# A two-layer graph network on one core: split aggregate, another order of first slot and drain, first load in halves

## Chip, core and metric

One core of a Trainium2 chip runs the whole kernel. The metric is the device time of one execution in microseconds.

## What is computed

64 graphs of 128 nodes with 256 features, in fp32. Each graph goes through two attention layers, each with a residual and a layer norm:

```python
# layer 0
q, k = split(x @ Wqk); v = x @ Wv0
agg = einsum('bij,bjd->bid', adj, k * mask)
w = 1/16 * mask * einsum('bid,bid->bi', q, agg)
x1 = layernorm(x + softmax(w, axis=1)[:, :, None] * v)
# layer 1
query = x1 @ Wq.T + bq; key = x1 @ Wk.T + bk; value = x1 @ Wv.T + bv
weight = adj * exp(query @ key.T)
weight = weight / sum(weight, axis=2)
out = layernorm(x1 + weight @ value)
```

## The kernel before

The graphs are taken in 32 pairs. Weights are folded first: M0 = Wq0 Wk0^T / 16 and A = Wk1^T Wq1, so that layer 0 needs x M0 and x Wv0 (one product of 512 columns, `project_half`), the masked adjacency times x (`aggregate`), and layer 1 needs z = A x1 (`queries`), the scores (`scores`), the values (`values`) and the weighted sum (`attend`). Products that must be exact to nearly fp32 are made of three fp32r products: each operand is split into a high part, which is a cast to fp32r, and a low part, which is what is left. `split_half` (L747) issues hi x hi, hi x lo, lo x hi. `aggregate` (L758), `scores`, `attend` and the transposes are plain fp32 products; for fp32 of 256 columns the trace has two matmul records to a product.

The order is written by hand, for each engine on its own, in a function `slot(t, r)`. The slots -2 to 29 are run in turn, 4 to 27 as a loop unrolled by four, and `drain` comes behind them. In slot t the engines work on pairs t-1 to t+4 at once. TensorE's order in a slot (L884):

- transposes of x1 of pair t (L822)
- aggregate and projection, first graph, of pair t+2 (L765, L748 to L750)
- attend of pair t-1 (L845)
- projection, second graph, of pair t+2
- queries of pair t
- transpose of the row w of pair t+2 (L791)
- values and scores of pair t
- transpose of the softmax row p of pair t+2 (L797)

VectorE (L640): p_col copy and x1_sum of pair t+1 (L544, L549), edge of t-1 (L651: exp(scores) times adj, two inputs from SBUF), the high and low part of x1t (L537, L539), statistics and variance, row weights w of t+2 (L524), x2 of t-1 (L691), its statistics, the row maximum (L703), the reciprocal and the product p_row of t+2 (L711), the score bias of t (L717).

ScalarE (L448): exponentials of the scores of t-1 (L403), copy of x1t of t (L458), copy of agg of t+2 (L464), high part of xt of t+3 (L390), norm of x2 of t-3 and of x1 of t+1 (L396), z bias of t (L409), row exponential of t+2 (L490) into exp_row in SBUF, value copy of t (L503).

GpSimd (L328): rstd and shift of the two norms (L336, L339), low part of xt of t+3 (L344), x1b = x1 + value bias of t+1 (L275), mask of adjacency t+3 (L267).

SyncE issues all transfers in one queue. At the start: wqk (512 KB), xt(0), wv0, adj(0), x(0), the parameters of layer 1, and so on.

The words slot, pair and half are used in this sense below. PSUM has 8 banks: x1t and z share bank 0, scores and sums banks 1 and 2, the values 3 and 4, the projection 5 and 6 (with the rows w and p in the same banks), the aggregate 7.

```python
def split_half(out, s_hi, s_lo, m_hi, m_lo, first, last):
    nc.tensor.matmul(out, s_hi, m_hi, start=first, stop=False)
    nc.tensor.matmul(out, s_hi, m_lo, start=False, stop=False)
    return nc.tensor.matmul(out, s_lo, m_hi, start=False, stop=last)
```

## Time and profile before

| | |
|---|---|
| median of 3 runs | 312.04 us (311.88 to 312.27) |
| profiled execution | 311.97 us, span 310.1 us |
| TensorE matmul busy | 298.0 us, 96% |
| weight loads busy | 269.3 us, 87% |
| VectorE | 223.6 us, 72% |
| ScalarE | 195.8 us, 63% |
| GpSimd | 143.2 us, 46% |
| 16 DMA engines | 32.8% of their time, 31.26 MB |

The span runs from the first to the last instruction; the run's own time has about 2 us around it. Matmuls overlap one another, so a matmul's own length is more than its step to the next; the time that a series takes is read from starts. An engine's idle time is put down to what ended it, in square brackets.

### The profile page before, as it was taken

The numbers are of one execution on the slowest core, as the hardware profiler recorded it, in microseconds if no ns is written. First come the engines' busy times: TensorE is split into PE (matmuls) and PEld (weight loads), VectorE is DVE, ScalarE is ACT, GpSimd is POOL, SyncE is SP. The second block draws the span as 40 slices with busy tenths as digits, with TensorE's granted clock in tenths as the row PEclk, the third lists the DMA queues.
The fourth block names the chain that finished last, engine by engine and source line by source line (L and its number), as shares of the span: only waits on it lengthen the run. The fifth ranks groups of instructions, "written<-read, shape, count | busy, mean of one in ns | idle before, by whom it ended". The sixth has DMA issues, their size and how long they took to land. (4 is left out here: it accounts for less than half of the span.)

```text
span 310.1 us, 6526 instructions
## 1 busy us (share of the span) xinstructions
PE 298.0 (96%) x1900; PEld 269.3 (87%) x1900; DVE 223.6 (72%) x691; ACT 195.8 (63%) x453; POOL 143.2 (46%) x181
## 2 busy tenths in 40 slices
PE   8997999999999999999999999999999999999891
PEld 6876999999998999999998999999999999999780
DVE  2475778777778877777788777778877777788565
ACT  4354556676666666766666676666666766665761
POOL 2365554345555444455543345555443455542522
PEclk9999999999999999999999999999999999999997
DMA  6921224232434332234333222444423234210012
GB/s 231 327 71 35 85 88 116 52 113 83 118 119 119 119 91 80 80 105 119 119 119 111 83 73 90 118 119 119 119 85 83 81 107 119 85 53 36 34 36 101
DMA packets 19165, 31.26 MB, mean 101 GB/s; under 512 B 2128, under 2 KB 6608, under 8 KB 19152
## 3 DMA queue, kind: packets, MB, share of 16 engines
q1 hardware_dynamic: 19152, 31.11, 32.8%
q8 instruction: 6, 0.10, 0.1%
q14 instruction: 7, 0.06, 0.1%
HBM read 22.71 MB, written 8.39 MB: 100 GB/s over the span
## 5 line engine op out<-in xcount | busy, mean ns | idle before, releaser
L336 POOL TENSOR_TENSOR rstd<-var_eps,minus_half 128x4 f32<-128x4 f32 x31 | 31.5, 1018 | 138.6 <-DVE var_eps L669 124.5
L396 ACT ACTIVATE x<-x_sum,shift,rstd 128x256 f32<-128x256 f32 x62 | 34.0, 595 | 52.2 <-POOL shift L339 52.2
L748 PE MATMUL ps<-w_hi,xt_hi 128*128 128x512 f32 x128 | 61.6, 481 | 0.5 <-DVE w_lo L734 0.5
L750 PE MATMUL ps<-w_hi,xt_lo 128*128 128x512 f32 x128 | 50.4, 394 | 0.0
L749 PE MATMUL ps<-w_lo,xt_hi 128*128 128x512 f32 x128 | 50.2, 393 | 0.0
L275 POOL TENSOR_TENSOR x1b<-x,bv_all 128x512 f32<-128x512 f32 x32 | 41.5, 1297 | 4.3 <-DVE x L568 3.1
L344 POOL TENSOR_TENSOR xt_lo<-xt_raw,xt_hi 128x512 fp32r<-128x512 f32 x31 | 40.0, 1291 | 3.3 <-ACT xt_hi L390 3.3
L748 PE MATMUL ps<-wv_hi,x1t_hi 128*128 128x258 f32 x124 | 37.8, 304 | 0.0
L396 ACT ACTIVATE x<-x,shift,rstd 128x256 f32<-128x256 f32 x62 | 33.8, 595 | 3.5 <-POOL shift L287 3.5
L750 PE MATMUL ps<-wv_hi,x1t_lo 128*128 128x258 f32 x124 | 35.3, 285 | 0.0
L748 PE MATMUL ps<-x1t_hi,at_hi 128*128 128x256 f32 x124 | 35.1, 283 | 0.0
L749 PE MATMUL ps<-wv_lo,x1t_hi 128*128 128x258 f32 x124 | 35.1, 283 | 0.0
L749 PE MATMUL ps<-x1t_lo,at_hi 128*128 128x256 f32 x124 | 35.0, 282 | 0.0
L750 PE MATMUL ps<-x1t_hi,at_lo 128*128 128x256 f32 x124 | 34.8, 281 | 0.0
L409 ACT ACTIVATE z<-ps,z_bias 128x256 f32<-128x256 f32 x62 | 26.0, 470 | 11.3 <-PE ps L750 11.3
L524 DVE CUSTOM_DVE_ANT_0 agg<-ps,agg,adjt 128x256 f32<-128x256 f32 x64 | 30.9, 484 | 2.9 <-PE ps L750 0.8
L765 PE MATMUL ps<-x_raw,adjm 128*128 128x256 f32 x128 | 32.9, 380 | 0.0
L840 PE MATMUL ps<-x1t,z 128*128 128x128 f32 x240 | 31.8, 275 | 0.6 <-ACT z L409 0.6
L845 PE MATMUL ps<-val,edge 128*128 128x258 f32 x124 | 32.1, 380 | 0.0
L549 DVE SCALAR_TENSOR_TENSOR x_sum<-ps,p_col,x_raw 128x256 f32<-128x256 f32 x64 | 28.0, 479 | 3.2
L840 PEld LDWEIGHTS ps<-x1t,z 128*128 128x128 f32 x240 | 29.3, 191 | 0.8 <-ACT z L409 0.8
L748 PEld LDWEIGHTS ps<-w_hi,xt_hi 128*128 128x128 f32 x128 | 24.1, 188 | 5.7 <-issue 0.9
(121 smaller groups left out, 668.8 us busy)
## 6 DMA issues: line engine op xcount, KB each, us to landing
xt_raw<-xt_pairs SPq DMA_DIRECT2D x32, 256.0 KB, 2.7
x_raw<-x_pairs SPq DMA_DIRECT2D x32, 256.0 KB, 2.7
out_pairs<-x SPq DMA_DIRECT2D x31, 256.0 KB, 2.1
adjt<-adjt_pairs SPq DMA_DIRECT2D x32, 129.0 KB, 2.1
...
```

What stands on the lines that cost most here:

```text
L275: nc.gpsimd.tensor_tensor(x1b[r % 2][:, :].rearrange("p (g d) -> p g d", g=2), x1[r % 2][:, :].rearrange("p (g d) -> p g d", g=2), bv_all[ ...
L336: nc.gpsimd.tensor_tensor(rstd[r % 2][:, :, :], var_eps[:, :, :], minus_half[:, :, :], ALU.pow)\
L344: nc.gpsimd.tensor_tensor(xt_lo[(r + 3) % 2][:, :, :, :].rearrange("p t g n -> p (t g n)"), xt_raw[(r + 3) % 2][:, :], xt_hi[(r + 3) % 2][ ...
L396: last = nc.scalar.activation(out[:, graph(g)], in_[:, graph(g)], ACT.Identity, bias=shift[r % 2][:, layer, g:g + 1], scale=rstd[r % 2][:, ...
L524: nc.vector.tensor_tensor_reduce(agg[:, g, :], y_ps(r)[:, g, :], agg[:, g, :], adjt[r % 4][:, PAIR_N + g:PAIR_N + g + 1], 0.0, ALU.mult, A ...
L549: nc.vector.scalar_tensor_tensor(out=x1_sum[r % 2][:, graph(g)], in0=v0_ps(r)[:, g, :], scalar=p_col[:, g:g + 1], in1=x_raw[r % 4][:, grap ...
L748: nc.tensor.matmul(out, s_hi, m_hi, start=first, stop=False)
L749: nc.tensor.matmul(out, s_hi, m_lo, start=False, stop=False)
L750: return nc.tensor.matmul(out, s_lo, m_hi, start=False, stop=last)
L765: mm = nc.tensor.matmul(agg_ps[:, g, :], adjm[r % 2][:, graph(g, NODES)], x_raw[r % 4][:, graph(g)], start=True, stop=True)
L840: mm = nc.tensor.matmul(out[:, g, :], zs[:, k, graph(g, NODES)], xs[:, k, g, :], start=(k == 0), stop=(k == HALVES - 1))
L845: return nc.tensor.matmul(out[:, g, 0:VAL_COLS], edges[:, graph(g, NODES)], vals[:, g, :], start=True, stop=True)
```

## The change

It has four parts.

1. Split aggregate. For pairs 4 to 31 (SPLIT = 4) `aggregate` is a `split_product` of adjm and x. ScalarE makes the high parts (`split_adjm`, `split_x`), GpSimd the low parts (`low_adjm`, `low_x`), in new buffers. GpSimd's mask moves from the end of the slot to behind the shift. Pairs 0 to 3 keep the fp32 product.
2. First slot. The bias products, transposes of w and p, the z bias on ScalarE, the x1 transposes and GpSimd's x1b stand in another order in the start and in slot 0. The transposes of x1 are now issued at the end of a slot (`transpose_next`), which in other slots is the same place. exp_row lies in PSUM.
3. Drain. Pair 30 gets its own z, val and edge instead of pair 31, and its values, scores and attend come earlier.
4. First load. The host lays out wqk by halves of the contracted dimension, two transfers of 256 KB load it, and M0's products wait for the half that they need. ScalarE issues xt(0).

```diff
+SPLIT = 4
...
+        def exp_row_ps(r):
+            return yv_ps(r)[0:2, 0, NODES:2 * NODES]
...
-            sp.dma_start(p0[:, 0:4 * DIM], params0[:, 0:4 * DIM]).then_inc(wqk_loaded, 16)
-            load_xt(0, 0)
+            for k in range(HALVES):
+                c = graph(k, 2 * DIM)
+                sp.dma_start(p0[:, c], params0[:, c]).then_inc(wqk_loaded[k], 16)
...
+            def low_adjm(u, r):
+                pool.wait_ge(adjm_hi_done, u + 1 - SPLIT)
+                nc.gpsimd.tensor_tensor(adjm_lo[r % 2][:, :], adjm[r % 2][:, :],
+                                        adjm_hi[r % 2][:, :].bitcast(F32), ALU.subtract).then_inc(adjm_lo_done, 1)
+
+            def low_x(u, r):
+                pool.wait_ge(x_hi_done, u + 1 - SPLIT)
+                nc.gpsimd.tensor_tensor(x_lo[r % 2][:, :], x_raw[r % 4][:, :],
+                                        x_hi[r % 2][:, :].bitcast(F32), ALU.subtract).then_inc(x_lo_done, 1)
+
             def slot(t, r):
+                if exists(t + 3) and r + 3 >= SPLIT:
+                    low_x(t + 3, r + 3)
                 if exists(t + 1) or exists(t - 2):
...
+                if exists(t + 3) and r + 3 >= SPLIT:
+                    mask_adj(t + 3, r + 3)
...
                 if r == -2:
                     mask_adj(1, 1)
                     mask_adj(2, 2)
-                if r == -1:
                     pool.wait_ge(wv1_hi_done, 1)
                     nc.gpsimd.tensor_tensor(wv1_lo[:, :, 0:DIM], wv1T, wv1_hi[:, :, 0:DIM].bitcast(F32), ALU.subtract)\
                         .then_inc(wv1_lo_done, 1)
+                if r == -1:
+                    mask_adj(3, 3)
+                    pool.wait_ge(x1t_lo_done, 1)
                 if exists(t + 1):
...
-                if exists(t + 3) and r >= 0:
-                    mask_adj(t + 3, r + 3)
+                if exists(t + 3) and r + 3 >= SPLIT:
+                    low_adjm(t + 3, r + 3)
...
+            def split_x(u, r):
+
+                act.wait_ge(x_loaded[r % 4], transfers4(u, r))
+                act.wait_ge(agg_done, u - 1)
+                nc.scalar.copy(x_hi[r % 2][:, :], x_raw[r % 4][:, :]).then_inc(x_hi_done, 1)
+
+            def split_adjm(u, r):
+
+                act.wait_ge(adjm_done, u + 1)
+                act.wait_ge(agg_done, u - 1)
+                nc.scalar.copy(adjm_hi[r % 2][:, :], adjm[r % 2][:, :]).then_inc(adjm_hi_done, 1)
+
...
                 act.wait_ge(z_done, a + 1)
-                bias_z(z)
+                bias_z(z_a)
+                act.wait_ge(val_done, a + 1)
+                nc.scalar.copy(val_a[:, :, 0:DIM], val_ps[:, :, 0:DIM]).then_inc(val_copied, 1)
                 normed_out(DRAIN - 1, n + 1)
-
-                act.wait_ge(x1t_lo_done, b + 1)
-                nc.scalar.copy(x1t[:, :, :, :], x1t_drain_ps).then_inc(x1t_copied, 1)
-                act.wait_ge(val_done, a + 1)
-                nc.scalar.copy(val[:, :, 0:DIM], val_ps[:, :, 0:DIM]).then_inc(val_copied, 1)
-                act.wait_ge(z_done, b + 1)
-                bias_z(z_b)
                 act.wait_ge(score_done, a + 1)
                 act.wait_ge(score_bias_done, a + 1)
                 act.wait_ge(edge_done, a)
-                exp_scores(score_ps)
+                exp_scores(score_a_ps)
+
+                act.wait_ge(x1t_lo_done, b + 1)
+                nc.scalar.copy(x1t[:, :, :, :], x1t_drain_ps).then_inc(x1t_copied, 1)
+                act.wait_ge(z_done, b + 1)
+                bias_z(z)
                 act.wait_ge(val_done, b + 1)
-                nc.scalar.copy(val_b[:, :, 0:DIM], val_ps[:, :, 0:DIM]).then_inc(val_copied, 1)
+                nc.scalar.copy(val[:, :, 0:DIM], val_ps[:, :, 0:DIM]).then_inc(val_copied, 1)
                 act.wait_ge(score_done, b + 1)
                 act.wait_ge(score_bias_done, b + 1)
                 act.wait_ge(edge_done, b)
-                exp_scores(score_b_ps)
+                exp_scores(score_ps)
...
+                if r == 0:
+                    act.wait_ge(z_done, 1)
+                    act.wait_ge(biases_ready, 1)
+                    bias_z(z)
...
                                          accum_out=exp_sum[:, 0:1]).then_inc(row_exp_done, 1)
+                if exists(t + 3) and r + 3 >= SPLIT:
+                    split_adjm(t + 3, r + 3)
...
+                if exists(t + 4) and r + 4 >= SPLIT:
+                    split_x(t + 4, r + 4)
...
+            act.dma_start(xt_raw[0][:, :], xt_pairs[0]).then_inc(xt_loaded[0], 16)
...
                 sum_x1(b, b)
+                bias_scores(DRAIN)
...
+                bias_scores(a)
                 dve.wait_ge(sum_done, DRAIN + 1)
                 attended(DRAIN, sum_ps)
-                bias_scores(a)
+                weigh_edges(a, edge_a)
                 dve.wait_ge(x2_done, DRAIN + 1)
                 both_stats(1, x2[DRAIN % 4]).then_inc(stats2_done, 1)
                 dve.wait_ge(stats2_done, DRAIN + 1)
                 dve.wait_ge(shift_done, n + 1)
                 variance(1)
-                weigh_edges(a, edge)
-                bias_scores(b)
-                weigh_edges(b, edge_b)
 
                 dve.wait_ge(sum_done, a + 1)
-                attended(a, sum_ps)
+                attended(a, sum_a_ps)
                 dve.wait_ge(x2_done, a + 1)
                 both_stats(1, x2[a % 4]).then_inc(stats2_done, 1)
                 dve.wait_ge(stats2_done, a + 1)
                 dve.wait_ge(shift_done, n + 2)
                 variance(1)
-
-                dve.wait_ge(last_sum_done, 1)
-                attended(b, sum_b_ps)
+                bias_scores(b)
+                weigh_edges(b, edge)
+
+                dve.wait_ge(sum_done, b + 1)
+                attended(b, sum_ps)
...
-                    dve.wait_ge(bias_done, 1)
-                    nc.vector.tensor_copy(z_bias[:, :], bias_ps[:, 0:HALVES])
-                    nc.vector.tensor_copy(s_bias[:, :], bias_ps[:, HALVES:HALVES + 1]).then_inc(biases_ready, 1)
...
+                if r == -1:
+                    dve.wait_ge(bias_done, 1)
+                    nc.vector.tensor_copy(z_bias[:, :], bias_ps[:, 0:HALVES])
+                    nc.vector.tensor_copy(s_bias[:, :], bias_ps[:, HALVES:HALVES + 1]).then_inc(biases_ready, 1)
...
-                    nc.vector.tensor_scalar(p_row[0:2, :], exp_row[:, :], inv_sum[:, 0:1], None, ALU.mult)\
+                    nc.vector.tensor_scalar(p_row[0:2, :], exp_row_ps(r + 2), inv_sum[:, 0:1], None, ALU.mult)\
...
+                if r < SPLIT:
+                    pe.wait_ge(adjm_done, u + 1)
+                    pe.wait_ge(x_loaded[r % 4], transfers4(u, r))
+                else:
+                    pe.wait_ge(adjm_lo_done, u + 1 - SPLIT)
+                    pe.wait_ge(x_lo_done, u + 1 - SPLIT)
                 if exists(u - 1):
                     pe.wait_ge(agg_copied, u)
                 for g in range(2):
-                    mm = nc.tensor.matmul(agg_ps[:, g, :], adjm[r % 2][:, graph(g, NODES)], x_raw[r % 4][:, graph(g)],
-                                          start=True, stop=True)
+                    n = graph(g, NODES)
+                    if r < SPLIT:
+                        mm = nc.tensor.matmul(agg_ps[:, g, :], adjm[r % 2][:, n], x_raw[r % 4][:, graph(g)],
+                                              start=True, stop=True)
+                    else:
+                        mm = split_product(agg_ps[:, g, :], [(adjm_hi[r % 2][:, n], adjm_lo[r % 2][:, n],
+                                                              x_hi[r % 2][:, graph(g)], x_lo[r % 2][:, graph(g)])])
...
+                    if r == 2 and g == 0 and k == 0:
+                        transpose_p(1, 1)
...
                 values(x1t_hi_a, x1t_lo_a, 0)
+                values(x1t_hi_a, x1t_lo_a, 1).then_inc(val_done, 1)
...
-                values(x1t_hi_a, x1t_lo_a, 1).then_inc(val_done, 1)
+                pe.wait_ge(z_copied, a + 1)
+                scores(score_a_ps, z_a, x1t_a)
 
                 pe.wait_ge(x1t_lo_done, b + 1)
-                pe.wait_ge(z_copied, a + 1)
                 queries(x1t_hi, x1t_lo)
-                pe.wait_ge(x2_done, DRAIN + 1)
-                scores(score_ps, z, x1t_a)
+                pe.wait_ge(edge_done, a + 1)
                 pe.wait_ge(val_copied, a + 1)
+                attend(sum_a_ps, edge_a, val_a, 0)
+                attend(sum_a_ps, edge_a, val_a, 1).then_inc(sum_done, 1)
                 pe.wait_ge(score_bias_done, a + 1)
                 values(x1t_hi, x1t_lo, 0)
                 values(x1t_hi, x1t_lo, 1).then_inc(val_done, 1)
                 pe.wait_ge(z_copied, b + 1)
                 pe.wait_ge(x1t_copied, b + 1)
-                scores(score_b_ps, z_b, x1t)
-                pe.wait_ge(edge_done, a + 1)
+                pe.wait_ge(x2_done, DRAIN + 1)
+                scores(score_ps, z, x1t)
+                pe.wait_ge(edge_done, b + 1)
+                pe.wait_ge(val_copied, b + 1)
                 attend(sum_ps, edge, val, 0)
                 attend(sum_ps, edge, val, 1).then_inc(sum_done, 1)
-                pe.wait_ge(edge_done, b + 1)
-                pe.wait_ge(val_copied, b + 1)
-                attend(sum_b_ps, edge_b, val_b, 0)
-                attend(sum_b_ps, edge_b, val_b, 1).then_inc(last_sum_done, 1)
+
+            def transpose_next(t, r):
+                pe.wait_ge(x1_done, t + 2)
+                if r == -1:
+                    pe.wait_ge(biases_ready, 1)
+                else:
+                    pe.wait_ge(z_copied, t + 1)
+                transpose_x1(x1t_ps, r + 1)
...
-                if r == 0:
-                    transpose_p(1, 1)
...
-                if exists(t + 2):
+                if exists(t + 2) and r > 0:
                     transpose_w(t + 2, r + 2)
...
+                    if r == 0:
+                        transpose_w(2, 2)
...
-                if exists(t + 2) and r != DRAIN:
+                if r == 0:
+                    transpose_next(t, r)
                     transpose_p(t + 2, r + 2)
+                elif r != DRAIN:
+                    transpose_p(t + 2, r + 2)
+                    transpose_next(t, r)
...
-            pe.wait_ge(wqk_loaded, 16)
             for m in range(HALVES):
                 for k in range(HALVES):
-                    mm = nc.tensor.matmul(m0_ps[:, m, :], wqkT[:, k, m * 128:(m + 1) * 128], wqkT[:, 2 + k, :],
+                    pe.wait_ge(wqk_loaded[k], 16)
+                    mm = nc.tensor.matmul(m0_ps[:, m, :], wqkT[:, 2 * k, m * 128:(m + 1) * 128], wqkT[:, 2 * k + 1, :],
...
-            fold_biases()
+            aggregate(1, 1)
             transpose_p(0, 0)
-            aggregate(1, 1)
             project(1, 1, 0)
             project(1, 1, 1)
+            fold_biases()
+            transpose_w(1, 1)
             aggregate(2, 2)
-            transpose_w(1, 1)
+            transpose_next(-1, -1)
```

On GpSimd, one slot of the loop. Before (rstd and shift of the norms, xt_lo of pair t+3, x1b of t+1, mask of t+3):

```order
L336 TENSOR_TENSOR rstd<-var_eps,minus_half 128x4
L339 TENSOR_TENSOR shift<-neg_mean,rstd 128x4
L344 TENSOR_TENSOR xt_lo<-xt_raw,xt_hi 128x512
L275 TENSOR_TENSOR x1b<-x_0,bv_all 128x512
L267 TENSOR_TENSOR adjm<-adjt 128x256
```

And now:

```order
L343 TENSOR_TENSOR x_lo<-x_raw,x_hi 128x512
L356 TENSOR_TENSOR rstd<-var_eps,minus_half 128x4
L359 TENSOR_TENSOR shift<-neg_mean,rstd 128x4
L275 TENSOR_TENSOR adjm<-adjt 128x256
L366 TENSOR_TENSOR xt_lo<-xt_raw,xt_hi 128x512
L283 TENSOR_TENSOR x1b<-x_0,bv_all 128x512
L338 TENSOR_TENSOR adjm_lo<-adjm,adjm_hi 128x256
```

Two subtractions are new, at the slot's two ends, and the mask stands ahead of xt_lo.

On ScalarE, from the copy of x1t(0) in slot 0 on. Before (z is the z bias, x_1 the norm of x1, exp_row the row exponential):

```order
L458 COPY x1t<-ps 128x512
L464 COPY agg<-ps 128x512
L390 CAST xt_hi<-xt_raw 128x512
L396 ACTIVATE x_1<-x_sum,shift,rstd 128x256 x2
L409 ACTIVATE z<-ps,z_bias 128x256 x2
L490 ACTIVATE exp_row,exp_sum<-ps,neg_max 2x128
L503 COPY val<-ps 128x2x256
L403 ACTIVATE exp_s<-ps,score_bias 128x128 x2
```

And now:

```order
L494 COPY x1t<-ps 128x512
L500 COPY agg<-ps 128x512
L414 CAST xt_hi<-xt_raw 128x512
L445 ACTIVATE z<-ps,z_bias 128x256 x2
L432 ACTIVATE x_1<-x_sum,shift,rstd 128x256 x2
L528 ACTIVATE ps,exp_sum<-ps,neg_max 2x128
L543 COPY val<-ps 128x2x256
L421 CAST x_hi<-x_raw 128x512
L439 ACTIVATE exp_s<-ps,score_bias 128x128 x2
```

The z bias stands ahead of the norm, and the cast of x ahead of the score exponentials. From slot 1 on the cast of adjm stands between the row exponential and the value copy as well.

On VectorE, the end of the drain (x_2 is x2 of pair 30, x_3 of pair 31). Before:

```order
L558 TENSOR_SCALAR neg_mean<-stats 128x2
L559 TENSOR_SCALAR var_eps<-stats 128x2
L555 TENSOR_TENSOR edge<-exp_s,adjt 128x256
L575 TENSOR_SCALAR score_bias<-ps,s_bias 128x2
L555 TENSOR_TENSOR edge_b<-exp_s,adjt 128x256
L563 RECIPROCAL den_inv<-ps 128x2
L568 SCALAR_TENSOR_TENSOR x_2<-ps,den_inv,x1b 128x256 x2
L530 BN_STATS stats<-x_2 128x6
L558 TENSOR_SCALAR neg_mean<-stats 128x2
L559 TENSOR_SCALAR var_eps<-stats 128x2
L563 RECIPROCAL den_inv<-ps 128x2
L568 SCALAR_TENSOR_TENSOR x_3<-ps,den_inv,x1b 128x256 x2
```

And now:

```order
L601 TENSOR_SCALAR neg_mean<-stats 128x2
L602 TENSOR_SCALAR var_eps<-stats 128x2
L606 RECIPROCAL den_inv<-ps 128x2
L611 SCALAR_TENSOR_TENSOR x_2<-ps,den_inv,x1b 128x256 x2
L573 BN_STATS stats<-x_2 128x6
L601 TENSOR_SCALAR neg_mean<-stats 128x2
L602 TENSOR_SCALAR var_eps<-stats 128x2
L618 TENSOR_SCALAR score_bias<-ps,s_bias 128x2
L598 TENSOR_TENSOR edge<-exp_s,adjt 128x256
L606 RECIPROCAL den_inv<-ps 128x2
L611 SCALAR_TENSOR_TENSOR x_3<-ps,den_inv,x1b 128x256 x2
```

The last edge product stands behind all of pair 30's work, and only its own den_inv and x2 follow it.

## Rows read from the trace of the kernel before

**Rows 1.** Stretches view: PE, PEld, DVE, ACT, POOL busy us, clock, DMA share, GB/s.
```profile
80.00:160.00 80.00, 80.00 (x520) 72.97 (x520) 60.49 (x189) 54.09 (x126) 38.13 (x44) 1.00 0.34 102
```

**Rows 2.** Timeline, TensorE, one slot of the loop (start, length, engine, line).
```profile
146.15 0.27 PE L797 MATMUL ps<-ident,p_row 128*128 128x128 f32 x1
...
151.20 0.28 PE L748 MATMUL ps<-x1t_hi,at_hi 128*128 128x256 f32 x1
...
152.63 0.27 PE L791 MATMUL ps<-ident,w_col 128*2 128x128 f32 x1
...
155.09 0.27 PE L797 MATMUL ps<-ident,p_row 128*128 128x128 f32 x1
...
155.63 0.38 PE L765 MATMUL ps<-x_raw,adjm 128*128 128x256 f32 x1
...
156.73 0.39 PE L749 MATMUL ps<-w_lo,xt_hi 128*128 128x512 f32 x1
...
156.96 0.40 PE L750 MATMUL ps<-w_hi,xt_lo 128*128 128x512 f32 x1
```

**Rows 3.** Timeline, GpSimd, ScalarE and the edge product, same slot.
```profile
150.05 1.02 POOL L336 TENSOR_TENSOR rstd<-var_eps,minus_half 128x4 f32<-128x4 f32 x1 [4.50 <-DVE var_eps L669]
...
153.81 0.61 POOL L267 TENSOR_TENSOR adjm<-adjt 128x256 f32<-128x256 f32 x1
...
153.81 0.18 ACT L490 ACTIVATION_READ_ACCUMULATOR exp_row<-ps,neg_max 2x1 f32 x1
...
154.40 0.59 ACT L503 COPY val<-ps 128x512 f32<-128x512 f32 x1 [0.41 <-PE ps L750]
...
155.32 0.62 ACT L403 ACTIVATE exp_s<-ps,score_bias 128x128 f32<-128x128 f32 x2 [0.34 <-PE ps L840]
...
156.46 0.41 DVE L651 TENSOR_TENSOR edge<-exp_s,adjt 128x256 f32<-128x256 f32 x1
```

**Rows 4.** Groups by form: line, shapes, count, busy us, mean ns of one.
```profile
L344 POOL TENSOR_TENSOR xt_lo<-xt_raw,xt_hi 128x512 fp32r<-128x512 f32 x31 | 40.0, 1291 | 3.3 <-ACT xt_hi L390 3.3
...
L390 ACT CAST xt_hi<-xt_raw 128x512 fp32r<-128x512 f32 x32 | 19.9, 623 | 3.8 <-DMA xt_raw<-xt_pairs 3.8
...
L510 ACT CAST w_hi<-p 128x256 fp32r<-128x256 f32 x2 | 0.7, 402 | 0.0
```

**Rows 5.** One line each, VectorE: shortest, median and longest ns, first and last start.
```profile
L734 DVE TENSOR_TENSOR w_lo<-p,w_hi x2: 415/624/834, 7.1 to 7.4; 128x256 fp32r<-128x256 f32 x2
...
L537 DVE CAST x1t_hi<-x1t x30: 418/420/1427, 20.9 to 282.1; 128x512 fp32r<-128x512 f32 x30
...
L711 DVE TENSOR_SCALAR p_row<-exp_row,inv_sum x32: 273/289/723, 13.6 to 288.5; 2x128 f32<-2x128 f32 x32
```

**Rows 6.** Timeline, ScalarE and TensorE, end of slot 0.
```profile
27.54 0.82 ACT L409 ACTIVATE z<-ps,z_bias 128x256 f32<-128x256 f32 x2
...
28.25 0.34 ACT L490 ACTIVATE exp_row<-ps,neg_max 2x128 f32<-2x128 f32 x1
...
29.77 0.30 PE L797 MATMUL ps<-ident,p_row 128*128 128x128 f32 x1 [0.21 <-DVE p_row L711]
...
30.36 0.38 PE L765 MATMUL ps<-x_raw,adjm 128*128 128x256 f32 x1
```

**Rows 7.** Timeline, TensorE and VectorE, the drain.
```profile
288.91 0.30 PE L797 MATMUL ps<-ident,p_row 128*128 128x128 f32 x1
...
289.73 0.22 DVE L717 TENSOR_SCALAR score_bias<-ps,s_bias 128x2 f32<-128x2 f32 x1 [0.96 <-ACT val L503]
...
302.08 1.14 PE L845 MATMUL ps<-val_b,edge_b 128*128 128x258 f32 x4 [0.33 <-DVE edge_b L555]
...
304.03 0.16 DVE L563 RECIPROCAL den_inv<-ps 128x2 f32<-128x2 f32 x1
```

**Rows 8.** Timeline, ScalarE and TensorE, the first projection.
```profile
6.63 0.71 ACT L510 CAST w_hi<-p 128x256 fp32r<-128x256 f32 x2
...
7.64 0.47 PE L748 MATMUL ps<-w_hi,xt_hi 128*128 128x512 f32 x1 [0.49 <-DVE w_lo L734]
```

45 lines of the change are left out of this document (18 added, 27 removed).

## The prediction

> **What bounds the kernel now.** I read the table of stretches first [rows 1]. TensorE is busy for the whole 80 us of a stretch in the middle; the list of waits names none of TensorE's between 40 and 270 us, and its clock there is granted in full. VectorE and ScalarE are busy three quarters and two thirds of that stretch, GpSimd under half. So in the loop only TensorE's own work counts, as long as no other engine becomes late. Second, one slot of the loop on TensorE [rows 2]: from one transpose of the softmax row (L797) to the next, 8.94 us. Third, the same slot on GpSimd and ScalarE, for their free time [rows 3]. Last, the two ends of the program, where TensorE does wait [rows 6 to 8].
>
> **The aggregate, 28 of 32 pairs.** Before, one aggregate is two fp32 products, four matmul records. The first starts at 155.63; the projection behind it has its second record at 156.73, and records of that shape follow at 0.23 us (156.73 to 156.96), so the projection began at 156.50: four passes take 0.87 us, 0.2175 each [rows 2]. After, it is six fp32r products of 128x256. Twelve of just that shape, the queries, run from 151.20 to 152.63: 0.119 each, six take 0.715 [rows 2]. Gain 0.155 us a slot. Pairs 4 to 31 are changed, so 28 x 0.155 = **4.3 us**, and the slot becomes 8.785 us. Everything else on TensorE in the loop stays in the same order: the x1 transposes stood behind the softmax transpose already, only in the next slot's text.
>
> **What pays for it on ScalarE.** Two casts a slot. The half of adjm (128x256) takes 0.40 us, of x (128x512) 0.62 [rows 4]. The first goes behind the row exponential, whose accumulator read ends at 153.99 (153.81 + 0.18), and before the value copy at 154.40, which waits for TensorE: 0.41 us are free and 0.40 wanted [rows 3]. The second goes behind the value copy (154.40 + 0.59), before the score exponentials at 155.32. Two copies follow each other about 0.1 us before the first has ended, so it runs about 154.9 to 155.5 and the exponentials start 0.1 us late. Behind them ScalarE waits for the aggregate anyway. I cost both at nothing. If that cover failed, the score bias and the column copy behind it on VectorE would be late, and with them x1_sum, for which the projection waits.
>
> **What pays for it on GpSimd.** The subtraction for x (128x512) costs 1.29 us, that for adjm half, 0.65 [rows 4]. GpSimd's new order is: low half of x, rstd, shift, mask, xt_lo, x1b, low half of adjm. The last is what the next aggregate waits for. From the start of rstd at 150.05 to that of the mask at 153.81 lie 3.76 us (rstd, shift, xt_lo, x1b) [rows 3]; with mask 0.61 and the new 0.65 the chain ends at 155.07. The aggregate's weights are wanted 0.1 us before its first pass, now at 146.15 + 8.785 + 0.54 - 0.1 = 155.38 (0.54 from L797 at 155.09 to L765 at 155.63) [rows 2]. So 0.3 us of slack, the narrowest place of the change. The low half of x ends soon after its cast, about 156.9, two microseconds before rstd of that slot; alone it costs nothing.
>
> It does collide with VectorE. Two VectorE subtractions of one shape at the start, with GpSimd's first mask beside them, took 415 and 834 ns; the cast of x1t takes 420 ns, and 1427 once, in slot 0, when GpSimd's x1b ran beside it; the p_row product 273 to 723 [rows 5]. The low half of x (155.6 to 156.9) lies over the edge product, which ran at 156.46 in this slot [rows 3]. Held until 156.9, that ends about 0.3 us later, with it x1t_hi, x1t_lo, the statistics, the variance and rstd: the slack of 0.3 is used up, to within a tenth. The page "SBUF — State Buffer" of the Trainium skill, section "Who interferes with whom", states it harder: a VectorE instruction with two SBUF inputs and a GpSimd one that reads SBUF exclude each other for the whole instruction. The pair 415/834 agrees with that. By the page the edge product waits for all that is left of the subtraction, which is what I have just counted. Taken as strictly for x1t_hi and x1t_lo it makes rivals 1 and 4, and by rival 1 the time would be 307.5 us instead of 304.7.
>
> I take no loss in the loop, with bounds of 0 and 2.8 us (a tenth of a microsecond in each of 28 slots). exp_row goes to PSUM and p_row is read from there. That is the same count of elements, and in the loop TensorE transposes p_row when its own order comes to it, not when p_row is ready: nothing for it there.
>
> **The start.** Before, the first aggregate of a full slot (pair 3) starts at 30.36 us, behind the transposes of p_row(2) at 29.77 and of x1 [rows 6]. What led to 29.77 was: x_sum(1), its statistics, norm of x1(1), then the z bias on ScalarE (27.54), then the row exponential (28.25), then p_row. The change shortens it four times. GpSimd's x1b now waits for x1t_lo, so x1t_hi isn't held: 1.43 to 0.42, 1.0 us [rows 5]. The z bias goes ahead of the norm, so the exponential follows the norm directly: 28.25 - 27.54 = 0.7 us [rows 6]. p_row, 723 ns in that slot, is no longer held by the mask: 0.45 us [rows 5]. The x1 transposes (0.4 us) are issued ahead of p_row's, in its wait. Against it: the projection of pair 3 must still wait for x_sum(2), which now starts after the short path; I take 0.3 us back. 1.0 + 0.7 + 0.45 + 0.4 - 0.3 = **2.3 us** (2.25, rounded). The w transpose, for which TensorE waited in slot 0, now stands behind the values and is covered by them; that is the same time and isn't counted twice. The bias matmuls go behind projection 1 and hide in TensorE's wait for w_col(1). Bounds: 1.5 (another wait takes one of the steps), 3.0.
>
> **The first loads.** The first half of wqk lands earlier and the fold M0 begins earlier. But the first projection (7.64) follows the cast of wv0 (6.63) and its subtraction [rows 8], and wv0's transfer is still third in SyncE's queue with the same bytes before or beside it, xt(0) now on ScalarE's. Nothing gained. Bounds -0.4 and +0.3: an issue's time either way.
>
> **The drain.** The last pair's result waits on VectorE today: its attend is four passes from 302.08 on, about 0.9 us, so done and visible at 303.2; but its den_inv starts at 304.03, behind pair 30's x2, statistics and variance [rows 7]. The new order gives pair 30 its own edge, z and val early and takes its x2 before the last edge: **0.7 us**, at most 0.8 from this. The other part: score_bias(29) at 289.73 stood before p_col, though p_row was transposed from 288.91 [rows 7]; that start comes 0.5 us earlier, but TensorE must then first finish values of pair 30 (now both graphs ahead of the x1 transposes), so little of it passes through. Bounds 0 and 1.3.
>
> **Sum.** 4.3 + 2.3 + 0.7 = 7.3 us. The profiled execution took 311.97 us, 0.07 under the median of 312.04; either way **304.7 us**. A measurement of this kernel tells about 0.2% (0.6 us) from no change. Own range of this case: gains of 9.3 (4.6 + 3.0 + 1.3 + 0.4) to 5.4: 302.7 to 306.6.
>
> **Rivals.**
> 1. *The aggregate waits for GpSimd's low half of adjm.* For it: slack of 0.3 us against a delay of 0.3. Against it: the chain starts with the softmax transpose that ends one slot and is waited for in the slot after the next transpose, so it spans two slots, and each loses half of what it is late by. 0.1 us a slot takes 2.8 of the 4.3 back: 307.5 us. Chance 0.18.
> 2. *The start stays as long*, since another chain (norm of x1, x_sum(2)) ends there as late as before: 304.7 + 2.3 = 307.0 us. Chance 0.07.
> 3. *The split saves nothing*: six weight loads instead of four, and the switch between fp32 and fp32r passes, cost the 0.155 us. The queries show the rate, but not between fp32 neighbours. 312.0 - 3.0 = 309.0 us. Chance 0.06.
> 4. *Slower: GpSimd becomes the bound.* The place is the low half of x. If x1t_hi or x1t_lo, not edge alone, is held by it for a full 1.29 us, rstd is late by that, and low adjm by 1.29 - 0.3 = 1.0. The chain spans two slots, so a slot loses 0.5: 8.785 + 0.5 = 9.28 against 8.94 is 0.34 x 28 = 9.5 us more, less 3.0 from the ends: 318.5 us. It decides as slower from 0.26 us lost in a slot (0.155 + 3.0/28), that is a delay over 0.8 us of that chain. Against it: the cast of x ends before the exponentials, so GpSimd has long begun. By the same section of the Trainium skill whoever starts first holds the port; here GpSimd starts first and is nearly done. Chance 0.05.
> 5. *No change*: rivals 1 and 3 together with a lost start. 312 us. Chance 0.02.
>
> The forecast has 0.62. Faster: 0.62 + 0.18 + 0.07 + 0.06 = 0.93; within 0.2%: 0.02; slower 0.05. The range holds the forecast's own without its utmost gain and reaches to rivals 1 and 2: 303.2 to 307.6 us.
>
> **What the new profile would show.** Right: L797's successor every 8.78 us in the middle; six fp32r records of 0.12 us for an aggregate; TensorE with no wait on GpSimd's adjm_lo or x_lo; the aggregate of pair 3 at about 28 us; den_inv of the last pair behind TensorE, not behind VectorE's own work. Wrong: idle of TensorE before the aggregate, released by GpSimd (rivals 1, 4); edge or x1t_hi in the loop of over 0.8 us; a slot still 8.94 us with TensorE busy throughout (rival 3); a first projection later than 7.9 us.

## The result, and the profile after

The changed kernel takes 305.15 us (median of 4 runs, 304.99 to 305.53), the kernel before 311.96 us in the same comparison; ratio 0.978, 95% interval 0.977 to 0.980. The forecast was 304.7 us in a range of 303.2 to 307.6. The profiled execution is the longest of the four, 305.53 us with a span of 303.7 us.

The table of stretches after the change, same stretch and columns as [rows 1]:

```profile
80.00:160.00 80.00, 80.00 (x546) 73.98 (x546) 62.84 (x190) 61.08 (x146) 56.90 (x65) 1.00 0.34 103
```

TensorE is still busy throughout, with more records (546 for 520). GpSimd has paid: 56.90 us for 38.13. The waits of 40 to 270 us (us in total, times, longest) name no TensorE wait; the first rows are

```profile
POOL rstd L356 <- DVE var_eps L713: 61.6, 26, 2.4
ACT x L432 <- POOL shift L359: 50.2, 26, 2.9
DVE inv_sum L752 <- ACT ps L528: 21.0, 26, 0.8
```

One slot of the loop on TensorE (timeline; start, length), to be set against [rows 2]. L851 is the transpose of p_row, L876 those of x1, and L791 to L793 the three lines of the split product:

```profile
142.54 0.27 PE L851 MATMUL ps<-ident,p_row 128*128 128x128 f32 x1
...
151.36 0.27 PE L851 MATMUL ps<-ident,p_row 128*128 128x128 f32 x1
151.47 0.60 PE L876 MATMUL ps<-ident,x 128*128 128x128 f32 x4
151.83 0.38 PE L791 MATMUL ps<-x_hi,adjm_hi 128*128 128x256 f32 x1
152.04 0.28 PE L792 MATMUL ps<-x_lo,adjm_hi 128*128 128x256 f32 x1
152.16 0.28 PE L793 MATMUL ps<-x_hi,adjm_lo 128*128 128x256 f32 x1
...
152.52 0.28 PE L793 MATMUL ps<-x_hi,adjm_lo 128*128 128x256 f32 x1
152.64 0.40 PE L791 MATMUL ps<-w_hi,xt_hi 128*128 128x512 f32 x1
152.88 0.40 PE L792 MATMUL ps<-w_lo,xt_hi 128*128 128x512 f32 x1
```

Five of the six products start 0.12 us before their successor, as forecast; the first has 0.21. Not all of that is the first product's own: its record starts 0.03 us behind that of the last of the four transposes (151.80), and transposes follow each other at 0.11 us. The whole place, from the last transpose's start to the second record of the projection, took 156.73 - 155.53 = 1.20 us before and takes 152.88 - 151.80 = 1.08 now. The slot takes 8.82 us. From the transpose of p_row(3) to that of p_row(30), 27 slots, before: (280.42 - 38.74) / 27 = 8.951 us; after: (274.90 - 36.60) / 27 = 8.826 us. So a slot gained 0.125 us, not 0.155. Most slots take 8.79 to 8.83 us; the five in which the loop turns (in which its body of four slots starts again) take 8.97, 8.92, 8.91, 8.89 and 8.89.

The same slot on GpSimd and VectorE, which answers to [rows 3]:

```profile
143.03 1.29 POOL L343 TENSOR_TENSOR x_lo<-x_raw,x_hi 128x512 fp32r<-128x512 f32 x1
143.90 0.71 DVE L695 TENSOR_TENSOR edge<-exp_s,adjt 128x256 f32<-128x256 f32 x1
...
146.72 1.02 POOL L356 TENSOR_TENSOR rstd<-var_eps,minus_half 128x4 f32<-128x4 f32 x1 [2.40 <-DVE var_eps L713]
147.82 0.20 POOL L359 TENSOR_TENSOR shift<-neg_mean,rstd 128x4 f32<-128x4 f32 x1
147.97 0.61 POOL L275 TENSOR_TENSOR adjm<-adjt 128x256 f32<-128x256 f32 x1
148.54 1.28 POOL L366 TENSOR_TENSOR xt_lo<-xt_raw,xt_hi 128x512 fp32r<-128x512 f32 x1
149.79 1.28 POOL L283 TENSOR_TENSOR x1b<-x,bv_all 128x512 f32<-128x512 f32 x1
...
151.03 0.74 POOL L338 TENSOR_TENSOR adjm_lo<-adjm,adjm_hi 128x256 fp32r<-128x256 f32 x1
```

The low part of x runs over the edge product, which ends 0.3 us late (0.71 for 0.41 us), and the low part of the masked adjacency ends at 151.77, 0.05 us before the aggregate's first weight load at 151.82. On this way the slack of 0.3 us is used up, as worked out.

The start, which answers to [rows 6], and the drain, to [rows 7]:

```profile
20.97 0.43 DVE L580 CAST x1t_hi<-x1t 128x512 fp32r<-128x512 f32 x1 [0.53 <-ACT x1t L494]
...
24.66 0.84 ACT L445 ACTIVATE z<-ps,z_bias 128x256 f32<-128x256 f32 x2 [2.72 <-PE ps L793]
25.63 1.09 ACT L432 ACTIVATE x<-x_sum,shift,rstd 128x256 f32<-128x256 f32 x2
26.63 0.30 ACT L528 ACTIVATE ps<-ps,neg_max 2x128 f32<-2x128 f32 x1
...
27.28 0.34 DVE L756 TENSOR_SCALAR p_row<-ps,inv_sum 2x128 f32<-2x128 f32 x1
...
27.77 0.30 PE L851 MATMUL ps<-ident,p_row 128*128 128x128 f32 x1 [0.25 <-DVE p_row L756]
27.91 0.88 PE L814 MATMUL ps<-x_raw,adjm 128*128 128x256 f32 x3
...
296.38 1.14 PE L899 MATMUL ps<-val,edge 128*128 128x258 f32 x4 [1.25 <-DVE edge L598]
...
297.56 0.17 DVE L606 RECIPROCAL den_inv<-ps 128x2 f32<-128x2 f32 x1 [1.23 <-PE ps L899]
```

p_row(2) is transposed at 27.77 (before 29.77), and the aggregate of pair 3 starts at 27.91. The last pair's den_inv now waits for TensorE; TensorE's last product itself waits 1.25 us for VectorE's last edge product, where it waited 0.33 before [rows 7]. Where the span's 6.4 us come from: up to p_row(3) 38.74 - 36.60 = 2.14, the 27 slots 241.68 - 238.30 = 3.38, and from p_row(30) to the end 29.68 - 28.80 = 0.88, of which 0.13 is the last split aggregate and 0.75 the new order (the spans are read to 0.1 us, so these last three numbers hold to about that). The 2.14 hold a loss: the first projection starts at 8.08 us, not 7.64 [rows 8], so the start without the first load gained 2.58. Behind the first projection the start repeats well: to p_row(3) it is 28.52 us here and 28.51 to 28.54 in a1, a2, b1, c1, e1, e2 and f1 below.

For the terms of the start two rows of the kernel before are needed beside [rows 6]:

```profile
20.90 1.43 DVE L537 CAST x1t_hi<-x1t 128x512 fp32r<-128x512 f32 x1
...
26.54 1.09 ACT L396 ACTIVATE x<-x_sum,shift,rstd 128x256 f32<-128x256 f32 x2 [4.67 <-POOL shift L339]
```

From the start of x1t_hi to that of the norm 4.66 us pass, 5.64 before: 0.98 gained. From the norm to the row exponential 1.00 for 1.71: 0.71. From there to the transpose of p_row(2) 1.14 for 1.52: 0.38. From there to the aggregate of pair 3 0.14 for 0.59: 0.45. And from that to p_row(3) 8.69 for 8.38: 0.31 taken back. These are the five terms forecast as 1.0, 0.7, 0.45, 0.4 and -0.3, together 2.21 for 2.25.

The rest of the 2.58 lies ahead of them. From the first projection to x1t_hi the kernel takes 12.89 us, 13.26 before, a gain of 0.37. Ahead of the transpose of p_row(0) stood the bias products (first two rows, before), and now stands the aggregate of pair 1 (third row):

```profile
13.26 0.95 PE L810 MATMUL ps<-p 128*128 128x1 f32 x8
14.07 0.58 PE L814 MATMUL ps<-p,bq_wide 128*128 128x1 f32 x4
```

```profile
13.70 1.02 PE L814 MATMUL ps<-x_raw,adjm 128*128 128x256 f32 x4
```

The transpose of p_row(0) starts at 14.51 and 14.56: 1.25 us behind the first bias product before, 0.86 behind the first pass of the aggregate now, 0.39 less.

### The profile page after: what moved, and what is told of

It is laid out like the page before. It is cut to its first block, busy times and chain, and to the rows that moved or that the text cites. A ratio compares the mean times of both kernels' runs of the same rounds, so it can differ in the third digit from the quotient of the medians.

```text
span 303.7 us, 6830 instructions
## 1 busy us (share of the span) xinstructions
PE 294.2 (97%) x1956; PEld 269.6 (89%) x1956; DVE 227.3 (75%) x691; ACT 215.1 (71%) x509; POOL 198.0 (65%) x237
## 4 chain that ended last, share of the span: by engine, by line
PE 91%; DVE 3%; issue 2%; ACT 1%; POOL 1%; POOLq 0%; DVEq 0%
PE ps L791 22%; PE ps L793 21%; PE ps L792 21%; PE ps L899 8%; PE ps L894 8%; PE ps L876 4%; PE ps L998 1%; PE ps L814 1%; PE ps L851 1%; PE ps L845 1%; DVE stats L573 1%; PE ps L1003 1%; DVE x L611 1%; PE ps L856 1%; POOL x1t_lo_a L304 0%
## 5 line engine op out<-in xcount | busy, mean ns | idle before, releaser
L791 PE MATMUL ps<-w_hi,xt_hi 128*128 128x512 f32 x128 | 56.9, 444 | 0.4 <-DVE w_lo L777 0.4
L793 PE MATMUL ps<-w_hi,xt_lo 128*128 128x512 f32 x128 | 50.3, 393 | 0.0
L343 POOL TENSOR_TENSOR x_lo<-x_raw,x_hi 128x512 fp32r<-128x512 f32 x28 | 36.1, 1290 | 3.4 <-ACT x_hi L421 2.1
L791 PE MATMUL ps<-wv_hi,x1t_hi 128*128 128x258 f32 x124 | 37.9, 305 | 0.0
L793 PE MATMUL ps<-wv_hi,x1t_lo 128*128 128x258 f32 x124 | 35.3, 285 | 0.0
L793 PE MATMUL ps<-x1t_hi,at_lo 128*128 128x256 f32 x124 | 34.9, 282 | 0.0
L791 PE MATMUL ps<-x1t_hi,at_hi 128*128 128x256 f32 x124 | 34.9, 281 | 0.0
L894 PE MATMUL ps<-x1t,z 128*128 128x128 f32 x248 | 32.7, 275 | 0.0
L894 PEld LDWEIGHTS ps<-x1t,z 128*128 128x128 f32 x248 | 30.4, 191 | 0.0
L793 PEld LDWEIGHTS ps<-w_hi,xt_lo 128*128 128x128 f32 x128 | 24.0, 188 | 5.4
```

Source lines behind the costliest of these rows:

```text
L343: nc.gpsimd.tensor_tensor(x_lo[r % 2][:, :], x_raw[r % 4][:, :], x_hi[r % 2][:, :].bitcast(F32), ALU.subtract).then_inc(x_lo_done, 1)
L894: mm = nc.tensor.matmul(out[:, g, :], zs[:, k, graph(g, NODES)], xs[:, k, g, :], start=(k == 0), stop=(k == HALVES - 1))
```

## The experiments

The numbers of slots and starts below are from one profiled execution each, the times are medians of 4 or 5 runs.

**The first load, in three variants.** In each, one or both of the change's edits there are put back:

```
a1_whole_sp:  sp.dma_start(p0[:, 0:4*DIM], ...); load_xt(0, 0); no load by ScalarE
a2_halves_sp: two halves, then load_xt(0, 0) on SyncE;          no load by ScalarE
a3_whole_act: sp.dma_start(p0[:, 0:4*DIM], ...);                act.dma_start(xt_raw[0] ...)
```

> The changed kernel with its first load put back: the 512 KB of Wq/Wk as one transfer, the first block of x behind it, both issued by SyncE. Measured beside it: changed kernel 305.15 us, first projection at 8.08 us (7.64 before the change). Theory (the new first load costs 0.44 us and nothing behind it hides that): first projection back at 7.6 to 7.7 us, time 304.7 us. Rival (the 0.44 us come from something else, such as the first masking or PE's clock early in the run): first projection still at 8.1 us, time 305.15 us.

> The changed kernel with the two halves of Wq/Wk kept, but the first block of x issued by SyncE behind both. If ScalarE's early block of x, sharing the DMA engines with the first half, is what costs: the first product starts earlier than at 4.66 us, first projection at 7.7 us or below, time 304.7 us or below. If the split into halves itself costs (two transfers, each with its own start): first projection stays at 8.0 to 8.1 us, time 305.15 us.

> The changed kernel with Wq/Wk as one 512 KB transfer again, and the first block of x still issued by ScalarE. The other half of the pair: if sharing with the block of x costs, first projection at 8.1 us or later and 305.15 us or more; if the halves cost, first projection at 7.6 to 7.7 us and 304.7 us.

| | time, us | ratio to before | first projection, us |
|---|---|---|---|
| changed kernel | 305.15 | 0.978 (0.977 to 0.980) | 8.08 |
| a1, both undone | 304.96 | 0.978 (0.977 to 0.979) | 7.71 |
| a2, halves only | 305.54 | 0.980 (0.978 to 0.981) | 8.04 |
| a3, ScalarE's issue only | 306.47 | 0.981 (0.979 to 0.983) | 8.94 |

By its one profile a1 says that the new first load costs 0.4 us. It doesn't bear that weight. Eight of the experiments below leave the changed kernel's first load alone (all but j2), and their first projections start at 7.58, 7.74, 7.90, 7.90, 7.93, 8.01, 8.15 and 8.24 us. A spread of 0.66 us is more than the 0.44 I read between before and after. The rows of M0 (timeline, TensorE), first of the kernel before, then of the changed kernel, then of h1:

```profile
4.67 2.48 PE L945 MATMUL ps<-p 128*128 128x256 f32 x8
```

```profile
4.66 3.04 PE L1003 MATMUL ps<-p 128*128 128x256 f32 x8
```

```profile
4.60 2.49 PE L1001 MATMUL ps<-p 128*128 128x256 f32 x8
```

The eight records start at nearly the same time and take 2.48, 3.04 and 2.49 us. Their own starts, read in narrow windows, show where the time goes. In each of these runs they follow each other at 0.42 to 0.43 us at first (the first step apart) and at 0.21 to 0.22 later, and what differs is the record at which the pace doubles: that at 5.69 us before, at 5.61 in h1, at 6.88 in the changed kernel, at 7.14 in a2. In a3 all eight are at the slow pace and take 3.78 us. So the first projection is late in the changed kernel's profile because TensorE kept its slow pace for longer there, and h1, with the same first load, did not. That is the rival that a1's expectation named, the clock early in the run: a factor of two lies between TensorE's two clock levels, 1.2 and 2.4 GHz. But the stretches view gives the granted clock as 1.00 from 4.5 to 7.5 us in all these runs, so its rows do not show that it is the clock, and what sets the moment was not tried.

The times say: both edits together cost 0.2 us or nothing (the intervals overlap). In a3's profile, with one 512 KB transfer and ScalarE's block beside it, TensorE waited 0.72 us for the weights and began M0 at 5.51; with halves M0 could begin at 4.66 us. Its median is 1.3 us above the changed kernel's, but two of its five runs took 305.40 us, less than any run of a2. The delay of the weights is thus seen in one execution, and its price is not shown.

**No low part of the adjacency** (the product takes the high part twice):

```
-  adjm_lo[r % 2] = adjm[r % 2] - adjm_hi[r % 2]       (GpSimd, each slot)
-  split_product(agg, adjm_hi, adjm_lo, x_hi, x_lo)
+  split_product(agg, adjm_hi, adjm_hi, x_hi, x_lo)
   (TensorE waits for adjm_hi in place of adjm_lo)
```

> The changed kernel without the low part of the masked adjacency: GpSimd's subtraction of 0.74 us per slot is left out, and the split products take the high part in its place, so the aggregate of pairs 4 to 31 is not the reference's; PE's instructions are the same. Theory (the aggregate now waits a few hundredths of a microsecond in most slots for GpSimd's low part, and that is the 0.04 us per slot that are missing from the forecast): mean slot down from 8.826 to 8.78 us, time 305.15 - 28 x 0.04 = 304.0 us. Rival (the product itself is longer than 1.57 - 0.155, or PE loses it elsewhere in the slot): mean slot 8.82 us, time 305.1 us. Second rival (GpSimd's work also holds VectorE's two-port operations, so that more than the wait goes): 303.5 us or below.

Measured: 305.20 us, 0.978 (0.977 to 0.980): my theory fell. The slots became even, 8.80 each where they had alternated by 0.02 to 0.04, but the mean moved from 8.826 to 8.818 only, and the slots at a turn kept their 8.90 to 8.94. The wait on GpSimd is worth 0.008 us a slot. TensorE itself needs 8.80 us. In its ordinary slots the place from the last transpose to the second record of the projection takes 1.07 us, 1.20 to 1.21 before: that is the slot's gain of 0.14.

**The same subtraction twice**, the opposite direction:

```
 def low_adjm(u, r):
     pool.wait_ge(adjm_hi_done, u + 1 - SPLIT)
+    spare[r % 2] = adjm[r % 2] - adjm_hi[r % 2]
     adjm_lo[r % 2] = adjm[r % 2] - adjm_hi[r % 2]
```

> The changed kernel with one more subtraction of 0.74 us on GpSimd per slot, directly ahead of the low part of the masked adjacency (into a tile nobody reads). Theory (GpSimd has no slack left on the way to the aggregate, which starts 0.05 us behind the low part): the aggregate waits for it in each slot. If the delay comes back in GpSimd's next slot only through the work that follows the aggregate, a slot grows by up to 0.74 us, 28 x 0.74 = 20.7 us, 326 us; if the chain back to itself spans two slots, by 0.37 us, 315.5 us. Rival (GpSimd's chain has slack elsewhere, its root waited 2.4 us in the slot shown): under 306 us.

Measured: 319.74 us, ratio 1.024 (1.023 to 1.026), 14.6 us more than the changed kernel, slower than before the change. The waits of 40 to 270 us now name TensorE and its weight loads:

```profile
PEld ps L794 <- POOL adjm_lo L341: 9.9, 18, 0.6
PE ps L794 <- POOL adjm_lo L341: 7.7, 24, 0.4
```

Its timeline shows why 0.74 us cost so much, first GpSimd from one low part of x to the next, then VectorE and TensorE's weight load:

```profile
149.76 1.31 POOL L346 TENSOR_TENSOR x_lo<-x_raw,x_hi 128x512 fp32r<-128x512 f32 x1
...
157.78 0.74 POOL L339 TENSOR_TENSOR spare<-adjm,adjm_hi 128x256 fp32r<-128x256 f32 x1
158.47 0.74 POOL L341 TENSOR_TENSOR adjm_lo<-adjm,adjm_hi 128x256 fp32r<-128x256 f32 x1
159.15 1.31 POOL L346 TENSOR_TENSOR x_lo<-x_raw,x_hi 128x512 fp32r<-128x512 f32 x1
```

```profile
150.18 1.17 DVE L698 TENSOR_TENSOR edge<-exp_s,adjt 128x256 f32<-128x256 f32 x1
...
159.26 0.19 PEld L794 LDWEIGHTS ps<-x_hi,adjm_hi 128*128 128x128 f32 x1 [0.59 <-POOL adjm_lo L341]
```

GpSimd now goes from adjm_lo straight to the next slot's low part of x (158.47 + 0.74 = 159.21, 159.15), and the profile lists no wait before any of its 28. From 149.76 to 159.15 are 9.39 us, and that is the slot: these two engines run in a loop of their own. The low part of x holds the edge product, which is done at 150.18 + 1.17 = 151.35, 1.59 us after the low part began; from there x1t_hi, x1t_lo, the statistics, rstd and the rest of GpSimd's order take 7.86 us to the end of adjm_lo. In the changed kernel the same two stretches take 1.58 (143.03 to 144.61) and 7.16 (144.61 to 151.77), 8.74 us in a slot of 8.82, and in 12 of its 28 slots the low part of x waits for its cast. So the loop had 0.1 to 0.2 us to spare; 0.70 were added, and the slot grew by 0.53, from 8.826 to 9.357. The edge product takes 1.17 us for 0.71 because the low part of x now begins 0.95 us after the transpose of p_row (149.76 - 148.81), not 0.49.

This is not the chain of the prediction's rivals 1 and 4. That chain spans two slots, and a slot would have lost half of what was added, 0.35 us. The loop through GpSimd's own order spans one, and loses all that exceeds its slack.

**The loop's gain, taken apart.** b1 leaves the split out whole; c1 keeps its casts, subtractions and waits, and multiplies in fp32.

```
b1_no_split:      SPLIT = 1000   (mask_adj stays where the change put it)
c1_fp32_product:  aggregate: if r < 1000: the fp32 product of adjm and x_raw
```

> The changed kernel with the aggregate in fp32 for all pairs and none of the preparation (no high and low parts of x and of the masked adjacency); start, drain and first load stay as changed. Theory (the split product is the whole of the loop's gain, 0.125 us per slot by the traces): mean slot 8.95 us as before the change, time 305.15 + 28 x 0.125 = 308.6 us. Rival (part of the loop's gain comes from the reordered transposes or from exp_row in PSUM): mean slot 8.90 us or less, time 307.5 us or less.

> The changed kernel with all the preparation of the split (two casts on ScalarE, two subtractions on GpSimd per slot) and its waits, but the product itself in fp32. Its difference to the kernel without preparation is the price of the preparation, its difference to the changed kernel the gain of the product. If preparation is hidden: the same time as without it, 308.6 us, mean slot 8.95 us. If the preparation takes 0.03 us of every slot from TensorE (the part of my 0.155 us that is missing): mean slot 8.98 us, 309.4 us.

Measured: b1 308.34 us, 0.988 (0.986 to 0.989), mean slot 8.941; c1 308.77 us, 0.989 (0.988 to 0.991), slots of 8.94 to 8.99 but for one. So the split product is worth 308.34 - 305.15 = 3.2 us, 0.114 a slot, and the preparation takes nothing of TensorE in an ordinary slot. That one took 9.49 us. In its waits between 78 and 93 us:

```profile
POOL adjm L275 <- DMA adjt<-adjt_pairs: 0.6, 1, 0.6
PEld ps L814 <- POOL adjm_lo L338: 0.5, 1, 0.5
```

The mask waited 0.6 us for its block of the adjacency, and all that stands behind it on GpSimd, adjm_lo at the end, was late by that. In b1 such a wait, 0.4 us before the mask at 274.72, cost nothing (that slot took 8.93), since TensorE there waits for no low part.

b1 also tells the turns apart. Its five slots at a turn take 8.93 to 8.96, no more than the rest (8.94). With the split product they take 8.92 on average against 8.805 for the rest, before the change 9.00 against 8.94. Thus the change gained 0.135 in an ordinary slot and 0.08 at a turn: 22 x 0.135 + 5 x 0.08 = 3.4 us. What the change does apart from the split (b1 against before) took the turns' 0.06 away, 0.01 a slot; i1 below makes it likely that exp_row's move did. The split brought 0.1 back, and by its product: with the casts and subtractions but the fp32 product (c1) the turns' slots take 8.94 to 8.99. The trace says where: from the last product of the aggregate to the second record of the projection an ordinary slot takes 152.88 - 152.52 = 0.36 us. A slot with a turn takes 126.45 - 125.99 = 0.46:

```profile
125.99 0.28 PE L793 MATMUL ps<-x_hi,adjm_lo 128*128 128x256 f32 x1
126.14 0.47 PE L791 MATMUL ps<-w_hi,xt_hi 128*128 128x512 f32 x1
126.45 0.39 PE L792 MATMUL ps<-w_lo,xt_hi 128*128 128x512 f32 x1
```

**No turn of the loop**, with a1's first load:

```
-LOOP_FROM, LOOP_TO, UNROLL = 4, 28, 4
+LOOP_FROM, LOOP_TO, UNROLL = 4, 28, 24
```

> Both kernels bettered, by what the runs so far point to: the changed kernel with its first load put back (304.96 us), and the loop body over 24 slots in place of 4, so that the program has no turn of the loop. In the changed kernel the five slots with a turn take 8.91 us on average against 8.80; with the fp32 aggregate they take no more than the others. Theory (it is the turn that costs 0.1 us, there being too little fp32 work to cover it): all slots 8.80 us, 304.96 - 5 x 0.1 = 304.4 us. Rival (longer code costs elsewhere what the turn did, as it has to be fetched as well): slots of 8.9 us scattered, 305.0 us or more.

Measured: 305.85 us (305.10 to 306.89), 0.980 (0.978 to 0.982), and both expectations were half right. The first 17 slots after p_row(3) took 8.79 or 8.80, those included that had held a turn: the turn does cost 0.1 us. But four of the last ten took 9.00 to 9.18. The waits of 196 to 260 us:

```profile
POOL adjm L274 <- DMA adjt<-adjt_pairs: 1.2, 3, 0.4
...
PEld ps L789 <- POOL adjm_lo L337: 1.0, 3, 0.4
```

It is c1's stall again: the 0.2 to 0.4 us by which a block of the adjacency is late reach TensorE almost in full. Its fastest run is no faster than the changed kernel's, and a1's 304.96 us is the best median measured; no kernel here beats the changed one by more than the measurement can tell.

**The start, step by step.** Each kernel takes one step of the change back:

```
g1_x1b_free:       GpSimd, slot -1:  - pool.wait_ge(x1t_lo_done, 1)
h1_z_behind_norm:  ScalarE, slot 0:  bias_z(z) behind norm(x1(1)) again
i1_exp_row_sbuf:   exp_row = sb("exp_row", [2, 128]) instead of exp_row_ps(r + 2)
```

> The changed kernel without GpSimd's wait for x1t_lo ahead of the first value-bias sum, so that this sum may run beside VectorE's x1t_hi of slot 0 again. My term of 1.0 us for the start rests on it. Theory: x1t_hi of slot 0 takes 1.4 us instead of 0.43, and the softmax transpose of pair 2 comes at 28.8 instead of 27.8 us, time 306.1 us. Rival (the path has room there, or the sum now starts early enough to be over): transpose at 27.8 to 28.0 us, 305.2 us.

> The changed kernel with the z bias of slot 0 behind the norm of x1 again, as in the other slots. My term of 0.7 us. Theory: the row exponential of slot 0 comes 0.7 us later, the softmax transpose of pair 2 at 28.5 us, time 305.85 us. Rival (the norm waits for the shift longer than the z bias takes, so that the order only matters by what is left): 0.2 to 0.4 us, 305.4 us.

> The changed kernel with exp_row in SBUF again, so that VectorE's product for p_row has its source in SBUF and may be held by GpSimd's subtractions. My term of 0.45 us at the start; I expected nothing from it in the loop. Theory: p_row has executions of 0.6 us or more, one of them in slot 0: transpose of pair 2 at 28.2 us; loop slots unchanged: 305.6 us. Rival (in the loop p_row now runs beside the low part of the adjacency and delays the softmax transpose): slots of 8.85 us or more, 306.5 us or more. Third case (p_row meets no GpSimd instruction any more): 305.15 us.

| | time, us | ratio to before | p_row(1) to p_row(2), us |
|---|---|---|---|
| changed kernel | 305.15 | 0.978 (0.977 to 0.980) | 6.93 |
| g1 | 305.63 | 0.979 (0.978 to 0.981) | 7.28 |
| h1 | 306.32 | 0.982 (0.980 to 0.983) | 8.09 |
| i1 | 307.24 | 0.984 (0.982 to 0.986) | 7.47 |

g1, timeline: x1b started at 20.02 and had 0.5 us left when x1t_hi began.

```profile
20.02 1.31 POOL L283 TENSOR_TENSOR x1b<-x,bv_all 128x512 f32<-128x512 f32 x1
20.82 0.80 DVE L579 CAST x1t_hi<-x1t 128x512 fp32r<-128x512 f32 x1 [0.52 <-ACT x1t L493]
```

x1t_hi took 0.80 us, not 1.43, so the wait is worth 0.35 us of the start, a third of my 1.0. x1b starts early here because another part of the change cleared its way: before, GpSimd did wv_lo (1.19 us, at 19.59) between xt_lo and x1b, which began at 20.73; now wv_lo is done at 14.9 and only a mask of 0.61 us stands there. h1 is worth more than its 0.7:

```profile
27.01 1.16 PE L892 MATMUL ps<-x1t,z 128*128 128x128 f32 x8 [1.32 <-ACT z L445]
28.01 0.60 PE L874 MATMUL ps<-ident,x 128*128 128x128 f32 x4
28.44 0.27 PE L849 MATMUL ps<-ident,p_row 128*128 128x128 f32 x1
```

z comes late too, the scores wait 1.32 us for it, and the transposes stand behind the scores. I had priced the row exponential alone. In i1 the start loses 0.54 us (I had 0.45), and then the loop:

```profile
L757 DVE TENSOR_SCALAR p_row<-exp_row,inv_sum x32: 274/616/875, 13.9 to 284.0; 2x128 f32<-2x128 f32 x32
```

(minimum, median and maximum in ns). From PSUM the product took 337 to 341 ns every time. Read from SBUF it is held by GpSimd's x1b (in the slot at 106.97 it ends at 107.66, x1b at 107.58); the ordinary slots stay at 8.80, but those with a turn go to 9.03 on average. I had given exp_row's move nothing in the loop.

**The old drain in the new kernel**:

```
-  scores(score_a_ps, z_a, x1t_a)  before queries(last pair); attend(pair 30) before values(last pair)
+  queries(last pair); scores(score_ps, z, x1t_a); values; scores(score_b_ps, z_b, x1t); attend(30); attend(31)
   (with the matching orders on ScalarE and VectorE, and the score bias of pair 29 in its slot)
```

> The changed kernel with the drain of before (the order of the last two pairs on all engines, z, values and edges of the last pair in buffers of their own, the score bias of pair 29 in its slot); split aggregate, start and first load stay. Theory (the new drain is worth 0.75 us): 305.9 us, last load-independent stretch from the softmax transpose of pair 30 to the end 29.5 us instead of 28.8. Rival (the drain's gain came from the split aggregate of pair 31 and from a slot that started sooner): 305.2 us.

Measured: 306.11 us, 0.981 (0.979 to 0.982). From the transpose of p_row(30) to the end 304.3 - 274.76 = 29.54 us against 28.80: 0.74 us, as expected; the medians differ by 0.96.

## Why the prediction was right, and where its terms were off

- **The aggregate: 4.3 us forecast, 3.2 to 3.5 measured.** The mechanism was right, the size too large: the 0.155 us a slot is the term that was mis-sized. An ordinary slot gained 0.135, and with no wait for adjm_lo (e1) 0.14. The six products run at the queries' rate, as assumed; some 0.02 us of the forecast are lost where they meet their neighbours, which the prediction took to be as close as before. The other part was not in the sum at all: a slot with a turn gained 0.08. The wait for adjm_lo, which I suspected first, is 0.008 us a slot (e1).
- **What pays for it.** ScalarE and GpSimd pay beside TensorE (c1 against b1). The slack of 0.3 us against a delay of 0.3 was right to 0.05 us. The rule that a slot loses half of such a delay was not: e2 lost 0.53 us a slot for 0.70 added, through a loop of one slot that the prediction did not have, GpSimd's low part of adjm into its next low part of x. Rival 4's outcome is what e2 shows, GpSimd as the bound and the kernel slower than before, by that loop and by the edge product and not by x1t_hi, which stayed at 415 ns there. That its time came near rival 4's 318.5 us is luck. What a delay of 0.1 or 0.2 us would cost, which rival 1 is about, was not tried.
- **The start: 2.25 forecast, 2.58 measured.** Read in place, the five terms are 0.98, 0.71, 0.38, 0.45 and -0.31, all within 0.1 of the forecast. What the forecast lacks is 0.37 ahead of them: it let the bias products hide behind projection 1 and counted nothing for the place that they left. Undone singly the steps are worth something else than in place: 0.35 (forecast 1.0), 1.16 (0.7) and 0.54 (0.45). The wait for x1t_lo is worth only 0.35, as without it x1t_hi already comes down from 1.43 to 0.80, wv_lo having moved; the z bias is worth 1.16, since z has two readers and I followed one. The 0.4 for the transposes, the 0.3 taken back and the bias products' 0.37 are read from the traces and were not tried by themselves.
- **The first loads: 0 forecast.** The profile shows -0.44, which comes from TensorE's slow pace lasting longer in that execution; the medians of a1 and the changed kernel differ by 0.2 or nothing. With 0 the parts make 3.5 + 2.58 + 0.75 = 6.83 us, and 311.96 - 305.15 is 6.81; parts of one execution and a difference of medians need not agree so closely.
- **The drain: 0.7 forecast, 0.75 and 0.74 measured.** den_inv behind TensorE is seen as foretold, but the drain still waits for VectorE, one step earlier: 1.25 us before the last attend.
- **exp_row in PSUM** was costed at nothing for the loop. i1 shows that without it each turn costs 0.1 us more (9.03 for 8.92). With the start's 0.54 that is the 1.1 us between the two profiled executions; the medians lie 2.1 apart, i1's runs spread from 306.09 to 307.73, and the rest is not explained.
- **The total.** 0.8 to 1.1 us too much for the aggregate was partly made up by 0.3 too little for the start, so the forecast of 304.7 lies closer to 305.15 than its largest term does. Of the signs of being wrong one came, a first projection later than 7.9 us (8.08), and it meant nothing, as the pace of M0 shows. The prediction's own range of 302.7 to 306.6 uses gains of 9.3 and 5.4 and doesn't say how its terms make them (4.3 + 1.5 + 0 - 0.3 is 5.5, and where 4.6 comes from is not given), and its bound of 2.8 us for the loop is in neither.
